# Spreading the first Wq, Wk and Wv scale rows by TensorE and sharing the parts of head 0 among three engines

## What is computed

```python
mod = (_silu(L0_c) @ L0_wmod).reshape(4, 6, 1, -1)
sa, ca, ga, sb, cb, gb = (mod[:, i] for i in range(6))
h = _layernorm(x) * (1 + ca) + sa
w = codes * jnp.repeat(scales, 32, axis=0)      # wq, wk, wv: 256x2048, scales 8x2048
q, k, v = h @ wq + bq, h @ wk + bk, h @ wv + bv  # 16 heads of 128
attn = softmax(q @ k.T / sqrt(128))
x = x + ga * ((attn @ v) @ wo + bo)
h = _layernorm(x) * (1 + cb) + sb
x = x + gb * ffn(h)                              # dense + top-2 of 8 low-rank experts
```

## Time and profile before

| what | value |
|---|---|
| median of 3 runs | 778.9 us (778.84 to 779.26) |
| the profiled execution's own time | 779.13 us |
| its span in the trace | 777.3 us |
| PE busy | 766.6 us (99%) |
| PE weight loads busy | 667.5 us (86%) |
| DVE busy | 629.8 us (81%) |
| ACT busy | 549.8 us (71%) |
| POOL busy | 563.3 us (72%) |
| chain that ended last, by engine | PE 90%, POOL 3%, DVE 2%, ACT 2%, the rest 1% each or less |
| mean granted TensorE clock | 0.998 |

### The profile page before, as it was taken

One profiled execution on the slowest core, in us unless ns is written; L12 is line 12 of the kernel. 1 busy time (PEld: TensorE's weight loads), 2 busy tenths in 40 slices (PEclk: granted clock), 3 DMA queues, 4 the chain that ended last, 5 costly groups with the idle time before them and its releaser, 6 DMA issues.

```text
span 777.3 us, 14887 instructions
## 1 busy us (share of the span) xinstructions
PE 766.6 (99%) x4206; PEld 667.5 (86%) x4206; DVE 629.8 (81%) x1190; ACT 549.8 (71%) x1188; POOL 563.3 (72%) x518
## 2 busy tenths in 40 slices
PE   7999999999999999999999999999999999999998
PEld 6888888888888888888888888888888888888887
DVE  5897888788788878888788878887888788879876
ACT  2798677767777776778677777777767776766841
POOL 4788796758767786777768686776778587899822
PEclk9999999999999999999999999999999999999999
DMA  7554365543454345544455434543455334433202
GB/s 217 164 147 126 93 146 150 140 111 96 116 145 131 95 98 137 131 120 99 111 136 143 98 94 125 142 126 93 102 140 152 95 93 108 110 87 89 49 1 109
DMA packets 71898, 90.68 MB, mean 117 GB/s; under 512 B 19573, under 2 KB 37430, under 8 KB 71866
## 3 DMA queue, kind: packets, MB, share of 16 engines
q1 hardware_dynamic: 53184, 74.00, 37.2%
q10 hardware_dynamic: 18682, 16.30, 7.1%
HBM read 22.06 MB, written 2.11 MB: 31 GB/s over the span
## 4 chain that ended last, share of the span: by engine, by line
PE 90%; POOL 3%; DVE 2%; ACT 2%; SPq 1%; DMA 1%; issue 1%; ACTq 0%; DVEq 0%
PE score L1105 9%; PE score L1106 9%; PE score L1107 9%; PE qv L1105 7%; PE o L1105 7%; PE qv L1106 7%; PE qv L1107 7%; PE o L1107 7%; PE o L1106 7%; PE ky L1105 4%; PE ky L1107 4%; PE ky L1106 4%; PE y L1107 2%; PE y L1106 2%; PE y L1105 2%; POOL pT_lo L406 1%
## 5 line engine op out<-in xcount | busy, mean ns | idle before, releaser
L406 POOL TENSOR_TENSOR pT_lo<-pT,pT_hi 128x512 fp32r<-128x512 f32 x248 | 314.5, 1305 | 165.4 <-ACT pT_hi L586 165.3
L947 DVE TENSOR_REDUCE neg_max<-score 128x1 f32<-128x512 f32 x256 | 174.3, 691 | 30.7 <-PE score L1107 30.1
L672 ACT ACTIVATE prob<-score,neg_max 128x512 f32<-128x512 f32 x256 | 174.6, 690 | 21.7 <-DVE neg_max L947 21.4
L960 DVE STREAM_TRANSPOSE pB<-prob 128x512 f32<-128x512 f32 x252 | 156.5, 677 | 0.3 <-ACT prob L672 0.3
L586 ACT ACTIVATE pT_hi<-pT 128x512 fp32r<-128x512 f32 x248 | 135.3, 620 | 0.0
L1105 PE MATMUL score<-k_hi,q_hi 128*128 128x512 f32 x256 | 101.3, 396 | 0.6 <-DVE k_lo L874 0.6
L1106 PE MATMUL score<-k_lo,q_hi 128*128 128x512 f32 x256 | 100.4, 392 | 0.0
L1107 PE MATMUL score<-k_hi,q_lo 128*128 128x512 f32 x256 | 99.7, 390 | 0.0
L1105 PE MATMUL o<-pT_hi,v_hi 128*128 128x512 f32 x248 | 96.9, 391 | 0.3 <-POOL pT_lo L406 0.2
L1107 PE MATMUL o<-pT_hi,v_lo 128*128 128x512 f32 x248 | 96.6, 390 | 0.0
L1106 PE MATMUL o<-pT_lo,v_hi 128*128 128x512 f32 x248 | 96.6, 390 | 0.0
(11 more groups left out here) (263 smaller groups left out, 1862.7 us busy)
## 6 DMA issues: line engine op xcount, KB each, us to landing
pT<-pB SPq DMA_DIRECT2D x1008, 64.0 KB, 2.0
out_dram<-x_nat SPq DMA_DIRECT2D x8, 256.0 KB, 2.1
stage<-in_L_attn_wv_codes_dram ACTq DMA_DIRECT2D x7, 256.0 KB
stage<-in_L_attn_wv_scales_dram ACTq DMA_DIRECT2D x14, 128.0 KB
stage<-in_L_attn_wq_codes_dram ACTq DMA_DIRECT2D x7, 256.0 KB
stage<-in_L_attn_wq_scales_dram ACTq DMA_DIRECT2D x14, 128.0 KB
stage<-in_L_attn_wk_codes_dram ACTq DMA_DIRECT2D x7, 256.0 KB
stage<-in_L_attn_wk_scales_dram ACTq DMA_DIRECT2D x14, 128.0 KB
```

The costliest lines, as they stand in the source:

```text
L406: pool.tensor_tensor(split(pT_lo, kt), turned(par, kt), split(pT_hi, kt).bitcast(f32), ALU.subtract).then_inc(p_lo_ok, 1)
L672: act.activation(prob[:, i], score_ps[i][:, :], ACT.Exp, bias=neg_max[:, i:i + 1], accum_out=row_sum[:, s % 2, i:i + 1]).then_inc(exp_ok, 1)
L947: dve.tensor_reduce(neg_max[:, i:i + 1], score_ps[i][:, :], AX.X, ALU.max, negate=True).then_inc(max_ok, 1)
L960: dve.transpose(pB[:, s % 2, :, i].rearrange("p g k q -> p k g q"), prob[:, i].rearrange("p (k g q) -> p k g q", k=QT, g=G)).then_inc(pB_o ...
```

## The change

The scales of Wq, Wk and Wv for the first pair are no longer loaded large. For each matrix one transfer brings 4 x 2 x 256 scales (8 KB) to 4 partitions, issued by ACT's queue ahead of the bias vectors. PE spreads them: a matmul with a 4 x 128 matrix of zeros and ones (`block_rows`, the identity's corner repeated over 32 columns) writes each scale to its 32 partitions, two matmuls of 256 columns per matrix, into the PSUM banks `o`, `y` and `score0`. DVE makes the products from PSUM (`first_product`): head 0 of Wq, head 0 of Wk, later all of Wv, and after the statistics of batch 1 head 1 of Wq and of Wk. Parts of head 0: Wq on POOL, Wk's high part on ACT and low part on DVE; of the input, the second high part moves from DVE to ACT. The bias columns move from DVE to ACT and the bias vectors' transpose on PE ahead of the input's. Normalising batch 1 moves from ACT to DVE, between the maxima and the turns of step 0, and its statistics are split around `k_low`. POOL loses two products and a shift, and makes Wv's parts second. The idle transposes go from 20, 14 and 10 to 4, 4 and 8. The queue of SP loses 12 transfers. What follows is the diff, cut.

```diff
+        block_rows = pB[0:NB, 0, 1, 0]
+        scale_rows = dict(q=gb_row[0:NB, 0:2], k=gb_row[0:NB, 2:4],
+                          v=pB[0:NB, 0, 0].rearrange("p i k q -> p (i k q)").rearrange("p (c n) -> p c n", c=2))
...
 
...
-            for a in range(NB):
-                src = bass.AP(SCALES[m].tensor, a * row, [[0, BLK], [half, 2], [1, PW]])
-                queue.dma_start(scales[m][at[a]:at[a] + BLK], src).then_inc(ld_w_first[m], 16)
+            if m == "o":
+                for a in range(NB):
+                    src = bass.AP(SCALES[m].tensor, a * D, [[0, BLK], [NB * D, 2], [1, PW]])
+                    queue.dma_start(scales[m][BLK * a:BLK * (a + 1)], src).then_inc(ld_w_first[m], 16)
+
+        def load_rows(queue, m):
+
+            src = bass.AP(SCALES[m].tensor, 0, [[FEAT, NB], [NB * FEAT, 2], [1, PW]])
+            queue.dma_start(scale_rows[m][:, :, :], src).then_inc(ld_rows[m], 16)
+
+        def first_scales(m):
+
+            return {"q": o_ps[0], "k": o_ps[1], "v": score_ps[0]}[m][:, :].rearrange("p (c n) -> p c n", c=2)
+
+        def head_cut(j):
+
+            return slice(None), slice(None), slice(j * HD, (j + 1) * HD)
 
...
@@ -380,15 +398,18 @@
                     cut, done = (slice(None), j, slice(None)), 2 * p + j
                 else:
                     cut, done = (slice(None), slice(None), slice(j * HD, (j + 1) * HD)), 2 * p + j
-                pool.wait_ge(w_prod[m], p + 1)
+                if isinstance(p, int) and p == 0 and m in "qk" and j == 0:
+                    pool.wait_ge(w_half[m], 1)
+                else:
+                    pool.wait_ge(w_prod[m], p + 1)
                 pool.tensor_tensor(w_hi[m][cut], w32[m][cut], one[:, 0:1].to_broadcast([P, PW]) if m == "o" else ones[:, 0:1].to_broadcast([P, 2, HD if m in "qk" else PW]), ALU.mult).then_inc(w_hi_ok[m], 1)
                 pool.wait_ge(w_hi_ok[m], done + 1)
                 pool.tensor_tensor(w_lo[m][cut], w32[m][cut], w_hi[m][cut].bitcast(f32), ALU.subtract).then_inc(w_ok[m], 1)
...
@@ -408,12 +429,9 @@
 
             inverse_std(0)
             parts("q", 0, 0)
-            product("k", 0)
-            parts("k", 0, 0)
+            parts("v", 0, 0)
+            inverse_std(1)
             parts("q", 0, 1)
-            inverse_std(1)
-            product("v", 0)
-            parts("v", 0, 0)
             parts("k", 0, 1)
             v_low(1, 0, 0)
...
 
         @block.scalar
         def _(act):
+            load_rows(act, "q")
+            load_rows(act, "k")
+            act.wait_ge(c_tr, 1)
+            act.activation(c_exp[:, :], qv_ps[:, 0:B * DC], ACT.Exp, scale=-1.0).then_inc(c_exped, 1)
+
+            load_rows(act, "v")
             for i, vec in enumerate((bq, bk, bv)):
                 act.dma_start(vec_raw[i * NH:(i + 1) * NH, :], vec.rearrange("(h p) -> h p", p=P)).then_inc(ld_vec, 16)
             act.wait_ge(bv_zero, 1)
             act.dma_start(bv_wo[0:1], bo.rearrange("(o d) -> o d", o=1)).then_inc(ld_bo, 16)
-            act.wait_ge(c_tr, 1)
-            act.activation(c_exp[:, :], o_ps[0][:, 0:B * DC], ACT.Exp, scale=-1.0).then_inc(c_exped, 1)
-
...
+            act.wait_ge(vec_tr, 1)
+            act.activation(vecT[:, NH:VECS], score_ps[1][:, NH:VECS], ACT.Copy).then_inc(vec_ok, 1)
+            act.activation(vecT[:, 0:NH], score_ps[1][:, 0:NH], ACT.Copy, scale=SCORE_SCALE).then_inc(vec_ok, 1)
+            act.wait_ge(vec_ok, 2)
+            act.activation(bias_now[:, 0:2], bias[:, 0:2, 0:2], ACT.Copy).then_inc(bias_ok, 1)
             act.wait_ge(mod_ok, 2)
...
             for c in range(DC):
                 input_high(0, c, score_ps[2 + c])
-            act.wait_ge(vec_ok, 2)
-            act.activation(bias_now[:, 0:2], bias[:, 0:2, 0:2], ACT.Copy).then_inc(bias_ok, 1)
+            act.wait_ge(h_ev, 2)
+            act.activation(hT_hi[:, 1, tokens(0)], hT32[:, 1], ACT.Copy).then_inc(h0_hi, 1)
+            act.wait_ge(w_half["k"], 1)
+            act.activation(w_hi["k"][head_cut(0)], w32["k"][head_cut(0)], ACT.Copy).then_inc(w_hi_ok["k"], 1)
             act.wait_ge(bias_ok, 1)
 
...
             q_high(1, 0)
             k_high(1, 0)
-            normalise(1, range(QT))
 
...
         @block.vector
         def _(dve):
 
+            dve.wait_ge(ident_ok, 1)
+            dve.tensor_copy(block_rows[:, :, :], ident[0:NB, 0:NB].unsqueeze(2).to_broadcast([NB, NB, BLK])).then_inc(block_ok, 1)
             dve.wait_ge(c_exped, 1)
             dve.tensor_scalar(c_exp[:, :], c_exp[:, :], 1.0, None, ALU.add).then_inc(silu_step, 1)
...
@@ -824,7 +853,10 @@
 
             def input_lo(b, c):
 
-                dve.wait_ge(h_hi, DC * b + c + 1)
+                if c:
+                    dve.wait_ge(h0_hi, 1)
+                else:
+                    dve.wait_ge(h_hi, 1)
                 dve.tensor_tensor(hT_lo[:, c, tokens(b)], hT32[:, c], hT_hi[:, c, tokens(b)].bitcast(f32),
                                   ALU.subtract).then_inc(h_lo, 1)
...
@@ -851,18 +883,25 @@
                 row_statistics(0, t)
             variances(0)
             normalise(0)
-            dve.wait_ge(ld_w_first["q"], LDW_FIRST)
-            dve.scalar_tensor_tensor(out=w32["q"][:, :, :], in0=codes["q"][:, :, :], scalar=SCORE_SCALE, in1=scales["q"][:, :, :],
-                                     op0=ALU.mult, op1=ALU.mult).then_inc(w_prod["q"], 1)
-            for c in range(DC):
-                input_hi(0, c)
-                input_lo(0, c)
-            dve.wait_ge(vec_tr, 1)
-            dve.tensor_copy(vecT[:, NH:VECS], o_ps[1][:, NH:VECS]).then_inc(vec_ok, 1)
-            dve.tensor_scalar(vecT[:, 0:NH], o_ps[1][:, 0:NH], SCORE_SCALE, None, ALU.mult).then_inc(vec_ok, 1)
+
+            def first_product(m, j):
+                dve.wait_ge(ld_w_first[m], 16)
+                dve.wait_ge(rows_mm[m], 1)
+                cut = head_cut(j) if m in "qk" else (slice(None), slice(None), slice(None))
+                dve.scalar_tensor_tensor(out=w32[m][cut], in0=codes[m][cut], scalar=SCORE_SCALE if m == "q" else 1.0,
+                                         in1=first_scales(m)[cut], op0=ALU.mult,
+                                         op1=ALU.mult).then_inc(w_half[m] if m in "qk" and j == 0 else w_prod[m], 1)
+
+            first_product("q", 0)
+            first_product("k", 0)
+            input_hi(0, 0)
+            input_lo(0, 0)
+            input_lo(0, 1)
+            dve.wait_ge(w_hi_ok["k"], 1)
+            dve.tensor_tensor(w_lo["k"][head_cut(0)], w32["k"][head_cut(0)], w_hi["k"][head_cut(0)].bitcast(f32),
+                              ALU.subtract).then_inc(w_ok["k"], 1)
+            first_product("v", 0)
             dve.wait_ge(vec_ok, 2)
-            dve.wait_ge(ld_x[1], 16)
-            statistics(1)
 
...
             q_low(1, slice(0, 1))
+            dve.wait_ge(ld_x[1], 16)
+            row_statistics(1, 0)
+            row_statistics(1, 1)
             k_low(1, slice(0, 1))
+            row_statistics(1, 2)
+            row_statistics(1, 3)
+            variances(1)
+            first_product("q", 1)
+            first_product("k", 1)
 
...
@@ -964,6 +1011,8 @@
                     maximum(1)
                     maximum(2)
                     maximum(3)
+                    if start:
+                        normalise(1)
                     if end:
                         inverse()
                         statistics(1)
...
             pe.wait_ge(ld_c, 16)
-            pe.transpose(o_ps[0][:, 0:B * DC], c_raw[:, :], ident[0:B * DC, 0:B * DC]).then_inc(c_tr, 1)
-
-            for i in range(20):
+            pe.transpose(qv_ps[:, 0:B * DC], c_raw[:, :], ident[0:B * DC, 0:B * DC]).then_inc(c_tr, 1)
+
+            for i in range(4):
                 pe.transpose(score_ps[0][:, (i % QT) * P:(i % QT + 1) * P], ident[:, :], ident[:, :])
+
+            def spread_rows(m):
+                pe.wait_ge(block_ok, 1)
+                pe.wait_ge(ld_rows[m], 16)
+                for c in range(2):
+                    ins = pe.matmul(first_scales(m)[:, c], block_rows[:, :, :].rearrange("a b q -> a (b q)"), scale_rows[m][:, c],
+                                    start=True, stop=True)
+                ins.then_inc(rows_mm[m], 1)
+
+            spread_rows("q")
+            spread_rows("k")
             pe.wait_ge(ld_wmod, 16)
             pe.wait_ge(silu_ok, 1)
             silu = c_silu[:, :].rearrange("p (b c) -> p c b", c=DC)
...
             def transpose_input(b):
-                if b == 0:
-                    pe.wait_ge(z_ok, QT)
+                if b < 2:
+                    pe.wait_ge(z_ok, QT * (b + 1))
                 else:
-                    pe.wait_ge(zin_ok, QT * b)
+                    pe.wait_ge(zin_ok, QT * (b - 1))
                 banks = INPUT_BANKS[b]
                 for c in range(DC):
...
+            pe.wait_ge(ld_vec, 16 * 3)
+            pe.transpose(score_ps[1][:, 0:VECS], vec_raw[:, :], ident[0:VECS, 0:VECS]).then_inc(vec_tr, 1)
             transpose_input(0)
```

(12 more changed lines are left out.)

23 lines of the change are left out of this document (12 added, 11 removed).

## The result

The changed kernel takes **783.08 us** (median of 4 runs, 782.65 to 783.65) against 779.08 (778.84 to 779.43) for the kernel before on the same chip: ratio 1.0052, 95% interval 1.0040 to 1.0063. It is 4.0 us slower, where the prediction had 777.9 and a range up to 779.4. The profiled execution took 783.65 us, its span is 781.7 (777.3 before).

The account below looks back on a forecast made before the run. PE was taken to bound the kernel from its first score on, with DVE's list in step 0 cutting the 2.4 us earlier first score to 1.0 at step 1: 778.9 - 1.0 = 777.9 us, range 776.7 to 779.4 for 8 in 10.

Parts of the forecast that it names:

- What bounds, and where it counts: Whole kernel: PE sets the time from its first score on; the loop and the end do not change.
- Loads of scales leave the path: Start: codes and scales come early enough for DVE, free at 9.6; its 1.14 us wait and POOL's until 14.28 go.
- Loads costed at nothing: Start: small rows and later bias vectors cost nothing; late bias vectors would shift what follows by 0 to perhaps 1 us.
- The cover that I named: Start: PE is held until the rows of z are there at 9.6 anyway; cover called thin for the bias vectors.
- Modulation and input transposes at the clock of before: Ahead of Q: eight input transposes end at 10.75, Wv's scales 1.8 us, 4 idle transposes, Q starts at 13.4.
- Clock back for the projections: Head 0's Q and K: clock back near 13.7, matmuls at 0.24 us, last K at 16.2; 0.43 each would be wrong.
- T: End of the first k_low in step 0: 20.3 us before the change, forecast at 17.95.
- DVE's list: Step 0, k_low to next q_lo: DVE's work sums to 9.9 us, so step 1's scores come only 1.0 us earlier.
- SP's transfers as a cap: Step 0: SP's 16 transfers start at 26.4 instead of 26.5, capping the gain at about 1.5 us.
- the clock stays low: Rival, start: scale matmuls and 4 transposes may not restore the clock; 778.9 to 781.4 us, chance 0.20.
- the stretch is as full as before: Start, the point against the low-clock rival: real matmuls run in between, where idle transposes were removed.
- The Trainium skill's rule on transposes: Start: the page says transposes do not raise the clock, so removing 32 would cost nothing; the trace disagreed.

Follow-up runs that it names:

- a3: Changed kernel with DVE doing batch 1's statistics ahead of q_low and its normalising between q_low and k_low: 781.95 us, ratio 1.0037 to the kernel before.
- g2: g1 with the normalising of batch 1 moved back from DVE to ACT: 778.42 us, ratio 1.0005 to the kernel before.
- b1: Kernel before with its 20, 14 and 10 idle transposes cut to 4, 4 and 8: 780.10 us, ratio 1.0016.
- b2: Kernel before with the first 20 and 14 idle transposes replaced by 10 and 7 fp32 matmuls over 4 partitions: 781.22 us, ratio 1.0027.
- d1: Changed kernel with fp32r scale rows, all scale matmuls behind input transposes, 28 and 14 idle transposes, products together, statistics ahead of q_low: 781.34 us.
- a1: Changed kernel with the 20, 14 and 10 idle transposes put back, nothing else: 785.05 us, ratio 1.0077 to the kernel before.
- f1: Changed kernel with fp32r rows, Wv's scale matmuls behind K's projection, Wq's and Wk's behind 20 idle transposes, DVE and bias transpose reordered: 779.85 us.
- h1: g2 with Wk's codes also held until the modulation matrix landed, Wq's and Wk's scale matmuls ahead of the modulation: 777.46 us, ratio 0.9979.
- d4: d1 without the rounding, scale matmuls in fp32: 784.26 us, ratio 1.0062 to the kernel before.
- g1: f1 with loads behind Wk's codes held until the modulation matrix landed, Wq's and Wk's scale matmuls behind the modulation, 14 idle transposes ahead of Q: 780.46 us.
- g3: g2 with the scale matmuls in fp32 on unrounded rows: 780.84 us, ratio 1.0032 to the kernel before.
- h2: h1 with Wq's and Wk's scale matmuls behind the modulation instead of ahead of it: 779.07 us, ratio 0.9998 to the kernel before.

## Why the prediction was wrong

- **What bounds, and where it counts: right.** PE's stream sets the time, and the time follows step 1's scores through 19 kernels: the span less that mark is 746.7 to 747.4 in all.
- **Loads of scales leave the path: right.** Neither DVE nor POOL waits for them.
- **Loads costed at nothing: wrong.** I looked at the bias vectors; what came 1.0 us later was the modulation matrix, beside which x, Wk's and Wv's codes now travel. The cover that I named (PE held until z at 9.6) is only the 0.5 us that PE had waited for z behind the modulation.
- **Modulation and input transposes at the clock of before: the step that failed.** I moved Q's start from 13.96 to 13.4 by counting records behind 10.75, and took the time up to there as unchanged, so the slower clock stood in the sum at nothing. The input transposes began at 11.97, not 9.67: the matrix 1.0 us later, the modulation 1.6 us longer (3.58 instead of 1.95), the bias vectors' transpose, moved ahead of them, 0.3, less the 0.5 of cover. The input transposes took 0.8 us more than I had, and Wv's scale matmuls 2.0, where I had 1.8. Q starts at 16.63 instead of 13.4.
- **Clock back for the projections: the same step, wrong again.** Instead of one slow matmul, the twelve matmuls start 0.43 us apart (the second 0.57 behind the first), up to 21.47: another 2.0 us. That is what I had named as a sign of being wrong. T is 23.45 where I had 17.95, and these 5.5 us are the 5.5 between step 1's scores at 34.96 and at 29.45, and the 5.2 between 783.08 and 777.9. The low clock makes 4.4 of them (1.6, 0.8 and 2.0).
- **DVE's list: right.** 9.84 us against my 9.9: statistics and gathering 1.28 (1.22 taken), products 0.67 (0.84), maxima 2.40 (2.66), normalising 2.07 (1.67), turns 2.40 (2.41), the rest 1.02 (1.09). PE waited for q_lo 0.91 us and, ahead of K's projection, 0.52 for ACT, more than a microsecond as said, and a3 and g2 show the list's price: 1.8 and 1.1 us.
- **SP's transfers as a cap: not tested.** They start at 32.37 now, with everything else behind them.
- **The rival "the clock stays low": it is what happened, and it had 0.20.** It named the rows that showed it and the cause, matmuls over 4 partitions and too few transposes. b1 shows the second alone (1.1 us), b2 the first (2.2 us). The point against it, "the stretch is as full as before", was the error of thought: from 2.9 to 16.6 us PE is recorded busy nearly all the time, but 5.8 us of that are over 4 partitions, and b2 shows that a full stretch of such matmuls can leave the clock low. Its terms, 2.3, 1.4 and 0.8, are near the measured 2.0, 1.6 and 0.8, but they add up to T = 22.45 and not to the 21.5 that it gave. That the matrix's 1.0 on top gives just the measured 23.45 is luck: the bias transpose, the cover and smaller terms cancel.
- **The Trainium skill's rule on transposes** ("TensorE: Matmul & The Clock Gate", on PE-mode transpose), which I set against the earlier trace rows: the runs agree with the row. In d1 and the kernel before, transposes end to end are followed by the modulation at 1.95 us, and the same places filled over 4 partitions (b2) by 3.58. By the page, the transposes should have done no more for the clock than b2's matmuls. They do not bring it in every execution: in a1's profile 20 of them, from 3.03 us on, were followed by no rise. (The change takes out 28 of the 44, not the 32 that I wrote.)

Between the two profiled executions lie 4.5 us (4.0 between the medians). Of these, 1.3 are step 0, mostly DVE's longer list (11.28 less 9.95). The first score is 3.2 later: at most 1.0 of it by the matrix, the rest by the clock and the scale matmuls, less what the shorter chain of loads gave. An exact split between clock and scale matmuls isn't to be had, because removing either changes the other.

Open: a timeline is there for one execution per kernel; of the others only the time and the mean granted clock are known, so where in them the clock rose and fell is inferred. Open is also why one and the same order gets the early rise in some executions and not in others (g2: six, two and three of its 11).

## What to carry to other kernels

Before replacing a filler or a wait on TensorE by useful work, ask what clock that filler holds, and what shape the new work has: small matmuls over few partitions can fill its time and leave what stands behind them at 1.2 GHz (b2, and the changed kernel). Keep such work short and put it where little follows at risk, or behind a stretch of full matmuls or transposes: in the profiles of f1 and h1, 0.7 and 1.0 us of it behind 20 transposes left the modulation at 1.95 us. Look at more than one execution, since one profile shows one case of the clock (a1, d4). When a load becomes small and so the ones behind it are issued earlier, look up which large load now lands later, and hold them back if it is on the path.

## What the runs showed of the hardware

- Matmuls over 4 of 128 partitions, 8.0 us of them in two stretches, did not raise the clock (b2: first rise at 21.7 us, 6.9 in the kernel before with transposes, 15.0 in b1 with few transposes). All six executions of b2 have a mean granted clock of 0.999 or 1.000; 99 of 119 of the kernel before have 0.995 to 0.998.
- The 16 matmuls of 4 columns each take 1.95 us at 2.4 GHz and 3.58 at 1.2. Behind them the clock fell in most profiles: at 10.3 us in the kernel before, and in f1 too, where it stands at 0.50 from 12.0 to 13.6. In d4 it stayed up for 4.5 us more, until 14.9, so that they are the cause is not shown.

```profile
12.00:13.60 1.60, 1.60 (x8) 1.54 (x8) 1.56 (x3) 1.57 (x4) 0.86 (x2) 0.50 1.14 251
```

- An fp32 spreading of 4 x 512 scales takes 1.9 to 2.1 us at 1.2 GHz and 0.9 to 1.0 at 2.4 (d4: 12.54 to 13.40 from start to start, the one ahead of it 0.97); on rows rounded to fp32r 0.4 to 0.6 (d1, start to start) and 0.35 (f1).
- The four normalising instructions took 2.15 us in step 0 and 1.67 ahead of it, on the same data sizes; the four maxima took 2.73 in a3 and 2.48 in the changed kernel.
- PE could start on the modulation matrix at 8.2 us in the changed kernel and 8.8 in a3, with all loads issued at once, and at 7.2 in the kernel before. With x of batch 1 and all later loads held back it was 8.0, 8.2 and 7.6 (g1, g2, g3), so single executions differ by over half a microsecond. With Wk's codes held back too, the next load, which waits for the matrix, went out at 7.3 (h1) and 7.4 (h2).
